# Layer 1's depthwise convolution in blocks of 4x28 from a two-half copy of x1, and the logarithm first in ScalarE's step

## What is computed

```
xs = silu(depthwise conv 5x5 of x1 + bias)            # per channel
dts, B, C = x_proj_w @ xs                             # 6 + 4 + 4 rows per image
delta = softplus(dt_w @ dts + dt_b)
log_dA = max(delta * A[n], LOG_EPS); P = exp(cumsum(log_dA))
h[n] = P * cumsum(delta * B[n] * xs / max(P, EPS))    # n = 0..3
y = sum_n h[n] * C[n] + xs * Ds
```

## Time and profile before

| | |
|---|---|
| median of 3 runs | 3910.67 us (3904.11 to 3912.43) |
| profiled execution, its own time | 3924.53 us |
| its span | 3922.7 us |
| granted TensorE clock, mean | 0.941 |
| PE busy | 3536.6 us (90%) |
| DVE busy | 3024.1 us (77%) |
| ACT busy | 2570.0 us (66%) |
| POOL busy | 2460.0 us (63%) |
| DMA | 383,903 packets, 613.00 MB |
| of these under 512 bytes | 200,064 |

### The profile page before, as it was taken

The page is one execution under the profiler, slowest core; times in us unless marked ns, Lnnn a source line. Parts: engine busy times, 40 slices in busy tenths (PEclk is TensorE's granted clock), DMA queues, the critical chain, the costliest instruction groups (busy, mean ns, idle before and its releaser), DMA issues.

```text
span 3922.7 us, 71069 instructions
## 1 busy us (share of the span) xinstructions
PE 3536.6 (90%) x22358; PEld 2662.2 (68%) x22358; DVE 3024.1 (77%) x3888; ACT 2570.0 (66%) x4292; POOL 2460.0 (63%) x2298
## 2 busy tenths in 40 slices
PE   6999999999999999997899898998989989899876
PEld 5878797978888797966766465565655656556422
DVE  3675847575675748473099899999999999999999
ACT  1462818274563718175588888788887888878865
POOL 0362716264452717173087888888888888888898
PEclk9999999999999999998899899998998989988888
DMA  7547474746556473525666465664756646565322
GB/s 220 174 123 231 97 255 99 231 115 194 165 137 211 97 259 96 194 64 127 167 170 178 129 180 141 167 181 122 192 149 164 183 123 189 149 166 162 103 79 62
DMA packets 383903, 613.00 MB, mean 156 GB/s; under 512 B 200064, under 2 KB 324320, under 8 KB 383216
## 3 DMA queue, kind: packets, MB, share of 16 engines
q1 hardware_dynamic: 383504, 607.96, 55.3%
HBM read 527.57 MB, written 80.28 MB: 155 GB/s over the span
## 4 chain that ended last, share of the span: by engine, by line
PE 33%; issue 8%; ACT 5%; POOL 4%; DVE 3%; DMA 1%; DVEq 0%; ACTq 0%; POOLq 0%; SPq 0%
PE ps_front L1315 11%; PE ps_y L1363 10%; PE ps_front L1308 4%; PE ps_prep L1337 3%; PE ps_y L1360 2%; PE ps_prep L1350 2%; PE ps_front L1328 2%; POOL h L1054 2%; DVE h L1140 1%; POOL u L1040 1%; ACT d_a L1226 1%; ACT d_a L1220 1%; DVE ps_q L1115 1%; POOL dxs L1028 1%; ACT xs L1184 1%
## 5 line engine op out<-in xcount | busy, mean ns | idle before, releaser
L322 POOL TENSOR_TENSOR h_low<-act_h,h_high 128x448 fp32r<-128x448 f32 x448 | 597.5, 1352 | 725.1 <-ACT h_high L521 724.8
L516 ACT ACTIVATE act_h<-ps_up,b 128x448 f32<-128x448 f32 x672 | 408.4, 633 | 729.2 <-PE ps_up L634 728.4
L1054 POOL TENSOR_TENSOR h<-h,c_rows 128x448 f32<-128x448 f32 x672 | 728.3, 1084 | 190.6 <-DVE h L1140 112.5
L1363 PE MATMUL ps_y<-h,ident 128*128 128x448 f32 x1344 | 689.9, 600 | 153.6 <-POOL h L1054 114.8
L1040 POOL TENSOR_TENSOR u<-dxs,b_rows 128x448 f32<-128x448 f32 x672 | 763.7, 1137 | 37.8 <-DMA bc_dram<-xd 21.7
L1115 DVE TENSOR_TENSOR_SCAN ps_q<-d_a,q_last,ps_q 128x450 f32<-128x450 f32 x576 | 661.5, 1148 | 1.3 <-ACT d_a L1226 1.3
L1140 DVE TENSOR_TENSOR_SCAN h<-d_a,h_last,ps_q 128x449 f32<-128x449 f32 x576 | 647.5, 1124 | 0.8 <-issue 0.7
L1315 PEld LDWEIGHTS ps_front<-win,taps 120*112 120x112 f32 x4608 | 535.2, 186 | 143.6 <-issue 141.0
L607 PE MATMUL ps_stage<-win,taps 124*112 124x112 f32 x6144 | 607.1, 260 | 2.7 <-DVE w_low L369 2.7
L607 PEld LDWEIGHTS ps_stage<-win,taps 124*112 124x112 f32 x6144 | 606.8, 178 | 3.2 <-DVE w_low L369 2.8
L1220 ACT ACTIVATE d_a<-delta,log_eps,a_neg 128x448 f32<-128x448 f32 x672 | 504.0, 751 | 97.4 <-DVE h L1140 55.8
(11 more groups left out here) (83 smaller groups left out, 6030.3 us busy)
## 6 DMA issues: line engine op xcount, KB each, us to landing
taps<-in_t_dram SPq DMA_DIRECT2D x192, 896.0 KB, 5.0
taps<-in_t_dram SPq DMA_DIRECT2D x192, 672.0 KB, 4.9
b_rows<-bc_dram SPq DMA_DIRECT2D x224, 224.0 KB, 3.0
c_rows<-bc_dram SPq DMA_DIRECT2D x224, 224.0 KB, 3.3
xres<-in_x_dram SPq DMA_DIRECT2D x224, 168.0 KB, 2.5
x_dram<-x1o SPq DMA_DIRECT2D x224, 168.0 KB, 2.0
x1pad<-x_dram SPq DMA_DIRECT2D x96, 392.0 KB, 5.8
out_dram<-y SPq DMA_DIRECT2D x168, 224.0 KB, 2.7
```

The costliest lines, as they stand in the source:

```text
L322: nc.gpsimd.tensor_tensor(h_low[u % 2][:, t, :], act_h[u % 2][:, t, :], h_high[u % 2][:, t, :], ALU.subtract).then_inc(h_low_ready[t], 1)
L516: nc.scalar.activation(act_h[u % 2][:, t, :], ps_up[t][:, 0:BT], ACT.Gelu, bias=b1[:, t:t + 1]).then_inc(gelu_done, 1)
L1054: nc.gpsimd.tensor_tensor(total, total, c_rows[n][:, :], ALU.mult).then_inc(hc_done, 1)
L1363: nc.tensor.matmul(total, ident[:, :], h[:, s % H_SLOTS, 0:BT], start=False, stop=(n == N - 1)).then_inc(y_added, 1)
```

## The change

Three parts belong together, and one stands alone.

1. **x1 in DRAM** gets another layout: for each channel and image two halves of 56 rows x 32 columns. Half 0 has columns 0 to 29 behind two zero columns, half 1 has columns 26 to 55 and then two zero columns. Layer 0's residual writes `x1o` in that form, in two instructions (columns 0 to 29 and 26 to 55), and its zero columns are set once by four memsets on POOL.
2. **A slab's load** copies, for each channel, two runs of 56 x 32 values into `x1pad`, now `[C, 2, 60, 32]`. It was 56 runs of 56 values.
3. **The convolution** works on patches of 4 x 28 pixels. A window is 4 x 32 = 128 pixels, two windows cover the six or more rows that a patch needs, so KT2 = 2, and a half has 15 windows. The number of transposes (30 a slab), of output columns (112) and of back transposes (4 a unit) stays. The back transposes write patches into their places in the band, 4 runs of 28.
4. **The logarithm** becomes the first operation of ACT's step, ahead of `clip_a`.

```diff
-COLS2 = W + 2 * PAD2
-WIN2 = ROWS * COLS2
-KT2 = (ROWS + K2 - 1) // ROWS
-NWIN2 = (H + 2 * PAD2) // ROWS
+PATCH_ROWS, PATCH_COLS = 4, W // 2
+PCOLS = PATCH_COLS + 2 * PAD2
+SEEN = PCOLS - PAD2
+WIN2 = PATCH_ROWS * PCOLS
+KT2 = (PATCH_ROWS + K2 - 1) // PATCH_ROWS
+ROW_BLK = H // PATCH_ROWS
+ROW_WIN = (H + 2 * PAD2) // PATCH_ROWS
+NWIN2 = 2 * ROW_WIN
+BAND_ROWS = BT // W
+BAND_BLK = BAND_ROWS // PATCH_ROWS
...
-        x1o = [sb(f"x1o{i}", [C, BT]) for i in range(2)]
+        x1o = [sb(f"x1o{i}", [C, 2, BAND_ROWS, PCOLS]) for i in range(2)]
...
-                sp.wait_ge(x1_done, g * UNITS + u + 1)
-                sp.dma_start(x1[ds((g * GI + u // BANDS) * C, C), (u % BANDS) * BT:(u % BANDS + 1) * BT],
-                             x1o[u % 2][:, :]).then_inc(x1_stored[u % 2], 16)
+                sp.wait_ge(x1_done, (g * UNITS + u + 1) * 2)
+                rows = slice(u % BANDS * BAND_ROWS, (u % BANDS + 1) * BAND_ROWS)
+                sp.dma_start(x1[ds((g * GI + u // BANDS) * C, C), :, rows, :].rearrange("c f h w -> c f (h w)"),
+                             x1o[u % 2][:, :, :, :].rearrange("c f h w -> c f (h w)")).then_inc(x1_stored[u % 2], 16)
...
-                nc.vector.scalar_tensor_tensor(x1o[u % 2][:, :], ps_down[u % 2][0:C, 0:BT], b2[:, 0:1],
-                                               xres[u % 2][:, :], ALU.add, ALU.add).then_inc(x1_done, 1)
+                total = ps_down[u % 2][0:C, 0:BT].rearrange("c (h w) -> c h w", w=W)
+                res = xres[u % 2][:, :].rearrange("c (h w) -> c h w", w=W)
+                for f, seen in enumerate((slice(0, SEEN), slice(W - SEEN, W))):
+                    nc.vector.scalar_tensor_tensor(x1o[u % 2][:, f, :, PAD2 * (1 - f):PAD2 * (1 - f) + SEEN],
+                                                   total[:, :, seen], b2[:, 0:1], res[:, :, seen],
+                                                   ALU.add, ALU.add).then_inc(x1_done, 1)
...
-                sp.dma_start(xpad[rows, PAD2:PAD2 + H, PAD2:PAD2 + W],
-                             x1img[ds((f * GI + k % GI) * C + CB * (k // GI), CB), :, :]
-                             ).then_inc(slab_ready[k % SLABS], 16)
+                sp.dma_start(xpad[rows, :, PAD2:PAD2 + H, :].rearrange("c f h w -> c f (h w)"),
+                             x1[ds((f * GI + k % GI) * C + CB * (k // GI), CB), :, :, :
+                                ].rearrange("c f h w -> c f (h w)")).then_inc(slab_ready[k % SLABS], 16)
...
+                    if (more or b + 1 < BANDS) and j - 1 in Z_AT:
+                        softplus(f, fb, Z_AT.index(j - 1), True)
                     if more or ahead < S:
                         clip_a(g, ahead)
...
-                        if j - 1 in Z_AT:
-                            softplus(f, fb, Z_AT.index(j - 1), True)
...
-                                win[cb % 2][:, k * CQ + c, :, w:w + IMG_BLK],
+                                win[cb % 2][:, k * CQ + c, :, :].rearrange("p i (f r) -> p (i f) r",
+                                                                           f=2)[:, :, w:w + ROW_BLK],
...
-                for j in range(BLKS):
-                    mm = nc.tensor.transpose(bank[i][:, j * TOK:(j + 1) * TOK],
-                                             conv[:, b * BLKS + j, t * 128:(t + 1) * 128], ident[0:TOK, 0:TOK])
+                pixels = bank[i][:, 0:BT].rearrange("p (r o f j) -> p r o f j", r=BAND_BLK, o=PATCH_ROWS, f=2)
+                for r in range(BAND_BLK):
+                    for f in range(2):
+                        mm = nc.tensor.transpose(pixels[:, r, :, f, :],
+                                                 conv[:, f * ROW_BLK + b * BAND_BLK + r, t * 128:(t + 1) * 128],
+                                                 ident[0:TOK, 0:TOK])
```

More of the change, by code:

```diff
@@ L100 @@
 assert TILES == CBS and GI * CB == 128
+assert PATCH_ROWS * PATCH_COLS == TOK and WIN2 == 128 and TURNS2 == 2 and TW2 == ROW_WIN
 def window_copy(win, ps_stage, n):
@@ L308, in _ @@
             nc.gpsimd.memset(minus_half[:, :], -0.5).then_inc(prepared, 1)
+            for i in range(2):
+                nc.gpsimd.memset(x1o[i][:, 0, :, 0:PAD2], 0.0).then_inc(prepared, 1)
+                nc.gpsimd.memset(x1o[i][:, 1, :, SEEN:PCOLS], 0.0).then_inc(prepared, 1)
             pool.sem_inc(x1_stored[0], 16)
@@ L1088, in _ @@
         def _(dve):
-            for border in (xpad[:, 0:PAD2, :], xpad[:, PAD2 + H:, :],
-                           xpad[:, PAD2:PAD2 + H, 0:PAD2], xpad[:, PAD2:PAD2 + H, PAD2 + W:]):
+            for border in (xpad[:, :, 0:PAD2, :], xpad[:, :, PAD2 + H:, :]):
                 nc.vector.memset(border, 0.0).then_inc(xpad_zero, 1)
@@ L1426, in banded, with patched @@
     return np.pad(t, ((0, 0), (0, 128 - ROWS * cols), (0, 0), (0, 0), (0, 0)))
+def patched(w):
+    t = np.zeros((C, KT2 * PATCH_ROWS, PCOLS, PATCH_ROWS, PATCH_COLS), np.float32)
+    for o in range(PATCH_ROWS):
+        for j in range(PATCH_COLS):
+            t[:, o:o + K2, j:j + K2, o, j] = w
+    t = t.reshape(QUNITS, CQ, KT2, WIN2, TOK).transpose(0, 3, 1, 2, 4)
+    return np.ascontiguousarray(t)
 def lay_out(i):
```

19 lines of the change are left out of this document (9 added, 10 removed).

## The result

The changed kernel takes 3882.85 us, the median of six runs (3870.71 to 3889.68), against 3909.99 for six runs of the kernel before beside them (3904.11 to 3918.24): a ratio of 0.9922, 95% interval 0.9905 to 0.9939. That is 27 us faster where 65 were forecast. The direction held and the size did not; the range (3800 to 3885) holds by 2 us, which is luck, as two of its terms missed in opposite directions. Two of the eleven executions of store_split, further down, were in a slower state of the chip and are left out of its median and ratio.

What follows compares the result with a forecast made beforehand. DVE was taken to bound layer 1's groups, with 100 us idle to win. Terms -28 - 13 - 12 - 22 + 10 = -65 took the profiled 3924.5 to 3859.5 and the median 3910.7 to 3846 us, range 3800 to 3885.

Steps and rivals of the forecast that it cites:

- The bound: Layer 1's groups: DVE sets the pace, so relieving other engines or queues returns at most its 100 us of idle time.
- Layer 0, +10: Layer 0's residual becomes two instructions; 60 existing PE waits for DVE each grow 0.16 us: +10 us, bounds 0 and +54.
- Where PE is never waiting it costs nothing: PE is the cover: Layer 0: the longer residual costs only at the 60 places where PE already waits for DVE, 0.16 us each.
- Stores of x1 ... zero: Layer 0: x1 stores in 1,024-byte runs with 14% more bytes cost zero, under 5 us without cover.
- The logarithm, -12: Fourth band of six groups: moving the logarithm first saves 1.9 us each, -12 us, bounds -5 and -14.
- The slabs, -28 and -13: Long-run slabs let c_rows land earlier: -28 us in the sixth bands of seven groups, -13 at six group starts.
- what is late next is the logarithm, and its chain starts with PE, which the convolution below relieves: Sixth band: with the stall of u gone, the logarithm is next; 4.0 of 3.04 + 2.32 us come back.
- The prologue, -22: Layer 1's prologue: a third off 24 convolution units, longer transposes, earlier constants: -22 us, bounds -12 and -32.
- The sum: Whole kernel: -28 - 13 - 12 - 22 + 10 = -65 us against the profiled execution, carried over to the median.
- ACT keeps the stalls: Rival: behind SiLU bursts ACT stays busy and DVE's waits move to the logarithm; -32 us, 3879, chance 0.18.
- its rival: Rival: less PE work lowers the granted clock until PE bounds the groups; at 0.74, +56 us, 3967; chance 0.05.
- Row against rule: Slab landing: long runs land in about 4.0 us, against a rule that 32 partitions reach only 8 of 16 ports.

Runs made afterwards that it cites:

- store_split: Changed kernel with one residual instruction of 448 elements into padded rows and two stores a unit cutting the halves in 128-byte runs: 3873.37 us, ratio 0.9913.
- half_resid: Changed kernel without the residual's second instruction, so layer 1 reads zeros in the right half of x1: 3855.29 us, ratio 0.9850.
- two_resid: Kernel before with layer 0's residual as two instructions of 224 elements instead of one of 448: 3947.98 us, ratio 1.0094.
- xres_first: Changed kernel with SP issuing the next load of xres ahead of the store of x1 in layer 0: 3903.03 us, ratio 0.9968.
- before_resid: Kernel before with layer 0's residual moved behind the norm's steps 2, 3 and 4 on DVE: 3880.52 us, ratio 0.9920.
- log_resid: Kernel before with only two order moves, the logarithm first in ACT's step and the residual behind the norm's steps: 3847.74 us, ratio 0.9830.
- log_back: Changed kernel with the logarithm back in its old place, leaving layout and convolution alone: 3910.28 us, ratio 0.9988.
- load_split: Changed kernel with x1 stored in rows of 60 by one residual and one store; two slab loads cut the halves in 128-byte runs: 3878.84 us, ratio 0.9914.
- load_split_resid: Changed kernel with x1 in rows of 60, halves cut by short-run slab loads, and the residual behind the norm's steps: 3849.20 us, ratio 0.9826.
- wide_rows: Kernel before with x1 in rows of 60, so a slab is one long run a channel; old three-matmul convolution kept: 3912.83 us, ratio 0.9996.
- log_c: Kernel before with the logarithm first and SP's loads of c_rows ahead of the same step's slabs: 3883.03 us, ratio 0.9915.
- c_first: Changed kernel with SP's loads of c_rows issued ahead of the slabs of the same step: 3878.35 us, ratio 0.9925.
- resid_last_c: Changed kernel with the residual behind the norm's steps and SP's loads of c_rows ahead of the slabs: 3859.13 us, ratio 0.9854.

## Why the prediction was right or wrong

**The bound** held: DVE's idle time in the groups went from 100 to 42 us (1669.00 - 1626.95), and that is 58 of the 61 us that they gained.

**Layer 0, +10, was mis-sized: it measured +34.** The instruction's 457 ns was right (455). The step that failed is "Where PE is never waiting it costs nothing: PE is the cover": I multiplied 0.16 us by the 60 waits that PE already had, but a longer DVE also makes new waits. They went from 23 to 65 at one line, from 37 to 47 at the other. Of 224 x 0.24 = 54 us, 23 to 26 were on the path by the rates of half_resid and two_resid. "Stores of x1 ... zero" failed as well, by about 10 us. How the store costs that is not shown: xres_first rules out that it is the order of the two transfers in SP's queue.

**The logarithm, -12, was mis-sized the other way: alone it measured -37 in the groups.** That is against the profiled execution of before; from before_resid to log_resid, the same edit, it is 1713 - 1691 = 22, and 27 us lie between the medians of the changed kernel and of log_back. (6 x 1.9 is 11, not 12; the sum keeps 12.) I counted only the fourth band and gave the waits of the sixth band and of the group's start to the slabs. In the earlier trace rows it has 26 waits, of which 6 entered that term.

**The slabs, -28 and -13, failed as a cause by themselves.** SP's hold, the issue of `c_rows` and the lead that absorbs the rest were right; the landing of `c_rows`, 9 us for 4.5, and of a slab, 5.2 for 4.0, were not. But "what is late next is the logarithm, and its chain starts with PE, which the convolution below relieves" is where the saving left: long slabs alone gave -3 in the groups, and -4 behind the moved logarithm. At the group's start 0.15 us came back of the 1.7 to 1.9 allowed for `c_rows`. Layout and convolution together, without the logarithm, gave -33; behind the moved logarithm only 1689 - 1674 (the mean of the five executions above) = 15. The parts do not add: each works on the same 83 us of idle time. The slabs' form does count beside the new convolution: with short loads (load_split, load_split_resid) the groups take 1690 and 1694 and the waits for u 39 us, for 1674 and some 20. These loads are shorter and more than the old ones, so 16 to 20 us is what the long form is worth at most.

**The prologue, -22, held**: it measured -19, 132 us for 152, with units of 1.73 us. But the kernels whose prologues do the old work have 146 to 155, 149 in the mean, and those with the new work 130 to 137, 133 in the mean, so 16 is the better figure.

**The sum** against the profiled execution was -65 and the two traces show -47. The forecast put the groups at -53, the prologue at -22 and layer 0 at +10; the traces show -61, -19 and +34. So layer 0 alone missed by 24, more than the whole 18, and the groups gave 8 more than forecast. The medians show -27, because the profiled execution of before lay 14 over its median and that of the changed kernel 5 under: the former's groups take 1726 us, where before_resid, two_resid and wide_rows, with the old order of the logarithm, have 1713 to 1723. I had carried the 14 us difference over to the median unchanged.

**The rivals.** "ACT keeps the stalls" gave 3879 and was nearest to 3883, and its mechanism was shown at a group's start in log_c, c_first and resid_last_c, and in part in wide_rows. What it did not have is the logarithm's own gain and layer 0's price, which nearly cancel: its number was near by luck. The clock did not make PE the bound over whole groups as its rival had it; it does so for part of the 14 to 51 us that it stays at 0.50 around a group's start. That rival's page, TensorE: Matmul & The Clock Gate, section "A second HAM failure mode: psum-queue depth-cycling" in the Trainium skill, would have the clock oscillate under frequent small idles. The trace agrees that it does: in the steps of half_resid's longest group stretches of 12 us stand at 1.00 with dips to 0.72. But DVE is busy for 12.00 of 12 us in the dips, so they cost nothing there; what costs is the long stretch at 0.50 that begins where the front work has ended.

**Row against rule.** I sided with the line through the earlier trace rows, 4.0 us a slab, and that step failed. The measured 5.2 us, beside 4.1 for taps of the same 448 KB into all 128 partitions, is in line with the rule of the Trainium skill, SBUF — State Buffer, section "Door 1: The DMA port swizzle". Its estimate was 2.1 us of transfer instead of half of that; the difference here is 1.1. It is not isolated: the two loads stand at different places in SP's queue and differ in run length, and wide_rows' slabs, 420 KB in one run a channel, landed in 4.7 us.

## What to carry to other kernels

Before a layout is changed to speed up a transfer, try the moves that only change an engine's order: here two of them, the logarithm first and the residual behind the norm's steps, give 0.983 on the old kernel, and the new layout and convolution add nothing that can be measured to it. A wait that a change removes is worth what stays gone, so ask which engine is late next, and test that by removing the one wait without the other (wide_rows, log_c). Cost a longer instruction on an engine that others wait for by the slack of every turn, not by the waits that already show: here 0.43 to 0.49 of the added time was on the path. And size terms by more than one execution, since here five executions of the same layer 1 varied by 22 us in its groups.

## What the hardware showed that I had not expected

- 448 KB into 32 partitions in two runs of 7,168 bytes a channel lands in 5.2 us, and into 128 partitions in 4.1. Shortening the runs to 128 bytes, as two loads of 224 KB, gave a median of 5.1 us each in load_split.
- With the same program the clock stays at 0.50 for 14 to 51 us from the end of one group into the next, and the group behind it lasts 237 to 250 us (half_resid, groups two to seven). During the longest stretch the chain that ended last runs through PE.
- Replacing an instruction of 448 elements (673 ns) by two of 240 (455 ns each) adds 0.24 us of busy time; two of 224 (437 ns each) add 0.20.
